# Another order for the attention steps of a fused attention and scan kernel

## The reference, cut to what matters

```
def _attn(a, sin, cos, ga, ba, gb, bb, Wq, Wkv, Wo, bo):
    an = _ln(a, ga, ba)
    bn = _ln(a, gb, bb)
    q = an @ Wq
    k, v = jnp.split(bn @ Wkv, 2, axis=-1)
    ...
    q = _rope(q, sin, cos)
    k = _rope(k, sin, cos)
    dots = jnp.einsum('bhid,bhjd->bhij', q, k)
    attn = jax.nn.softmax(dots, axis=-1)
    out = jnp.einsum('bhij,bhjd->bhid', attn, v)
    ...
    return jax.nn.elu(out @ Wo + bo)
...
return x + (xi + xj) / 2
```

## Time and profile before

| | us |
|---|---|
| median of 3 runs | 327.38 |
| lowest, highest | 326.32, 327.53 |
| the profiled execution | 327.32 |
| its span, first to last instruction | 325.2 |
| first scores, unit 0 | 22.66 |
| first scores of unit 6, of unit 14 | 70.61, 132.12 |
| POOL's first `a_msk` of the scan | 183.10 |

### The profile page before, as it was taken

How to read it: one execution, slowest core, us unless ns; L and a number is a source line. 1 busy time by engine, 2 the same in 40 slices (tenths; PEclk the granted TensorE clock), 3 DMA queues, 4 the chain that set the end, 5 groups by cost and what they waited for, 6 DMA issues and landing times.

```text
span 325.2 us, 7775 instructions
## 1 busy us (share of the span) xinstructions
PE 236.3 (73%) x3138; PEld 141.6 (44%) x3138; DVE 206.1 (63%) x333; ACT 173.1 (53%) x298; POOL 126.1 (39%) x104
## 2 busy tenths in 40 slices
PE   0386977958676865754865799997999848956764
PEld 0153644545444443533565165643544424434331
DVE  2696885828474755754374796999767965483422
ACT  2253655637574757446535844566557337723380
POOL 2416364405444242710040494754796832300000
PEclk9999978969997999795596999998999989997555
DMA  7611010243213133304045300000000000011002
GB/s 179 229 67 65 34 35 33 76 105 84 56 43 67 35 67 81 83 3 85 11 94 112 75 2 2 2 3 3 2 2 2 2 0 2 2 39 29 1 0 65
DMA packets 34243, 15.26 MB, mean 47 GB/s; under 512 B 31008, under 2 KB 31520, under 8 KB 34080
## 3 DMA queue, kind: packets, MB, share of 16 engines
q1 hardware_dynamic: 32480, 13.67, 16.7%
q10 hardware_dynamic: 1728, 1.10, 1.4%
HBM read 5.42 MB, written 2.10 MB: 23 GB/s over the span
## 4 chain that ended last, share of the span: by engine, by line
PE 36%; DVE 31%; ACT 16%; issue 13%; DMA 2%; ACTq 1%; DVEq 0%
PE ring L560 14%; PE score L560 9%; DVE s_max L1043 5%; PE ring L565 5%; DVE s_cen L1047 3%; PE p_turn L560 3%; PE oz L560 2%; DVE mix L1134 2%; DVE ln_s L837 2%; DVE rot_sin L1000 2%; DMA back<-x 2%; DVE rot_cos L1000 2%; DVE ln_v L857 2%; DVE xhat L872 2%; ACT wo_b L1250 2%
## 5 line engine op out<-in xcount | busy, mean ns | idle before, releaser
L1520 POOL TENSOR_TENSOR a_msk<-dt_fin,c_sb 128x512 f32<-128x512 f32 x32 | 40.0, 1251 | 25.0 <-DVE dt_fin L975 15.2
L1043 DVE TENSOR_REDUCE s_max<-score 128x16 f32<-128x1024 f32 x16 | 19.6, 1223 | 26.6 <-PE score L560 26.6
L1134 DVE TENSOR_TENSOR mix<-dec,g_m 128x512 f32<-128x512 f32 x32 | 31.5, 988 | 2.2 <-ACT dec L1377 1.5
L1295 ACT ACTIVATE prob_t<-p_turn 128x512 f32<-128x512 f32 x32 | 17.5, 592 | 25.2 <-PE p_turn L565 25.2
L880 POOL TENSOR_TENSOR k_rot<-rot_cos,rot_swap 128x512 f32<-128x512 f32 x7 | 8.9, 1270 | 43.3 <-DMA rot_swap<-rot_sin 39.0
L1505 POOL TENSOR_TENSOR dtx<-xv,dt_fin 64x512 f32<-64x512 f32 x16 | 19.8, 1240 | 13.2 <-PE p_turn L560 12.3
L1303 ACT ACTIVATE prob<-s_cen 128x1024 f32<-128x1024 f32 x16 | 16.9, 1057 | 13.9 <-DVE s_cen L1047 13.8
L560 PE MATMUL score<-a_msk,c_sb 128*128 128x512 f32 x44 | 24.3, 634 | 0.0
L560 PE MATMUL score<-k_bd,q_rot 32*64 32x128 f32 x512 | 22.9, 329 | 0.0
L560 PEld LDWEIGHTS p_turn<-mix,dtx 128*32 128x32 f32 x512 | 11.0, 109 | 27.4 <-issue 14.6
L892 POOL TENSOR_SCALAR k_bd<-k_rot,c_sb 128x512 f32<-128x512 f32 x14 | 22.1, 1588 | 0.7
(11 more groups left out here) (177 smaller groups left out, 567.8 us busy)
## 6 DMA issues: line engine op xcount, KB each, us to landing
rot_swap<-rot_sin SPq DMA_DIRECT2D x32, 128.0 KB, 2.1
p_sb<-params SPq DMA_DIRECT2D x1, 1520.0 KB, 9.7
x_tok<-x SPq DMA_DIRECT2D x16, 64.0 KB
attention_j_turned<-y_tok SPq DMA_DIRECT2D x16, 64.0 KB, 2.2
back<-attention_j_turned SPq DMA_DIRECT2D x16, 64.0 KB, 2.5
ut_a<-u SPq DMA_DIRECT2D x8, 126.0 KB, 2.8
ut_b<-u SPq DMA_DIRECT2D x8, 124.0 KB, 3.1
ut_b<-u SPq DMA_DIRECT2D x8, 122.0 KB, 3.2
```

The lines of the kernel that those rows point to most:

```text
L1043: v.tensor_reduce(s_max[:, n % 2, :], sc, AX, ALU.max).then_inc(s_maxed, 1)
L1134: v.tensor_tensor(mix[:, e % LAPS, :, :], dec[:, e % LAPS, :, :], wide(g_m[:, e // 4 % 2, e % 4, :], SSM_H), ALU.mult)\
L1295: a.activation(prob_t[:, e % 2, 4 * hp:4 * hp + 4, :].rearrange("p k n -> p (k n)"), PT[hp], ACT.Identity)\
L1520: gp.tensor_tensor(a_msk[:, m % LAPS, :, :], deep(dt_fin[:, 0, SSM_H * m:SSM_H * (m + 1)], GRID), wide(cst("tri"), SSM_H), ALU.mult).then_ ...
```

## The change

```
-ATT_STEPS = 25
+ATT_STEPS = 26
-XT_STEP = (13, 15, 17, 19)
-UT_STEP = (15, 17, 19, 21)
-XP_STEP = (17, 17, 18, 18, 20, 20, 21, 21)
+XT_STEP = (16, 17, 18, 20)
+UT_STEP = (18, 19, 20, 22)
+XP_STEP = (19, 19, 20, 20, 21, 21, 22, 22)
...
-        if odd:
-            uses = [("wo", g - 1), ("k", g + 2), ("yt", g - 2), ("vt", g + 1)]
+        elif odd:
+            a, b, c = [("vt", g + 1)], [("q", g + 2)], []
         else:
-            uses = [("q", g + 1), ("v", g + 1)]
+            a, b, c = [("wo", g - 2)], [("v", g + 1)], [("k", g + 2), ("yt", g - 3)]
...
-DT_STEP = 22
+DT_STEP = 23
...
                     last.then_inc(scored, 1)
+                for use in att_slots[n][0]:
+                    att_use(use)
...
-                for use in att_steps[n][:1]:
+                for use in att_slots[n][1]:
                     att_use(use)
...
-                for use in att_steps[n][1:]:
+                for use in att_slots[n][2]:
                     att_use(use)
...
-            ln_vector_b(v, 1)
             v.wait_ge(sin_signed, 1)
...
-                if use == ("k", 0):
+                if use == ("q", 0):
+                    ln_vector_b(v, 1)
                     ln_vector_c(v, 1)
-                if use == ("q", 0):
...
-                e = n - 1
+                e = n - 2
                 if 0 <= e < UNITS:
...
                     v.tensor_tensor(o_t[:, g % 2, CW // 2 * u:CW // 2 * (u + 1)], OUT, z_inv[:, e % 2, :], ALU.mult).then_inc(o_ready, 1)
+                if n < UNITS:
+                    v.wait_ge(s_maxed, n + 1)
...
+                    v.tensor_tensor(s_cen[:, n % 2, :, :], sc, deep(s_max[:, n % 2, :], GRID), ALU.subtract)\
+                        .then_inc(s_centred, 1)
...
-                if n % 2 == 0 and 1 <= n // 2 < ATT_CHUNKS:
-                    att_use(("vt", n // 2))
+                for use in att_slots[n][0] + att_slots[n][1]:
+                    att_use(use)
...
-                for use in att_steps[n]:
-                    if use[0] != "vt":
-                        att_use(use)
+                for use in att_slots[n][2]:
+                    att_use(use)
...
             copy_xn(0)
+            gp.wait_ge(mid_in, 16)
+            scale_weights(1)
+            gp.memset(v_bd[:, :, :, :], 0.0).then_inc(v_zeroed, 1)
             copy_xn(1)
```

More of the change, by code:

```diff
@@ L63 @@
 FOLD_STEP = 4
-XT_STEP = (13, 15, 17, 19)
-UT_STEP = (15, 17, 19, 21)
-XP_STEP = (17, 17, 18, 18, 20, 20, 21, 21)
+XT_STEP = (16, 17, 18, 20)
+UT_STEP = (18, 19, 20, 22)
+XP_STEP = (19, 19, 20, 20, 21, 21, 22, 22)
 def attention_uses():
-    steps = {-1: [("xr", 0), ("k", 0), ("q", 0), ("xr", 1), ("v", 0), ("vt", 0), ("k", 1)]}
+    steps = {-1: ([("xr", 0), ("k", 0), ("q", 0), ("xr", 1), ("v", 0), ("vt", 0)], [], [])}
     for n in range(ATT_STEPS):
         g, odd = divmod(n, 2)
-        if odd:
-            uses = [("wo", g - 1), ("k", g + 2), ("yt", g - 2), ("vt", g + 1)]
-        else:
-            uses = [("q", g + 1), ("v", g + 1)]
-        steps[n] = [(kind, c) for kind, c in uses if 0 <= c < (CHUNKS if kind == "yt" else ATT_CHUNKS)]
-        if n in (0, 2):
-            steps[n].append(("xr", 2 + n // 2))
+        if n == 0:
+            a, b, c = [("k", 1)], [], []
+        elif n == 1:
+            a, b, c = [("xr", 2), ("q", 1)], [("v", 1)], [("k", 2), ("xr", 3)]
+        elif n == 2:
+            a, b, c = [("vt", 1), ("q", 2)], [("v", 2)], [("k", 3)]
+        elif odd:
+            a, b, c = [("vt", g + 1)], [("q", g + 2)], []
+        else:
+            a, b, c = [("wo", g - 2)], [("v", g + 1)], [("k", g + 2), ("yt", g - 3)]
+        a, b, c = ([(kind, k) for kind, k in uses if 0 <= k < (CHUNKS if kind == "yt" else ATT_CHUNKS)] for uses in (a, b, c))
         if n == FOLD_STEP:
[L83 to L87, removed]
+            c.append(("fold", 0))
+        c += [("ut", q) for q in range(CHUNKS) if UT_STEP[q] == n]
+        c += [("xt", q) for q in range(CHUNKS) if XT_STEP[q] == n]
+        c += [("xp", k) for k, at in enumerate(XP_STEP) if at == n]
+        steps[n] = (a, b, c)
     return steps
@@ L151, in build @@
     lo, n_cols = offsets(COLS)
-    att_steps = attention_uses()
+    att_slots = attention_uses()
+    att_steps = {n: [use for slot in att_slots[n] for use in slot] for n in att_slots}
     ssm_before, ssm_steps = ssm_uses()
@@ L1030, in _ @@
                     q_sum(v, 0)
-                    ln_vector_b(v, 2)
                     v.wait_ge(bias_made, 2)
                     v.tensor_copy(b_att[:, 3:6], oz[:, 3:6]).then_inc(bias_here, 1)
-            ln_vector_c(v, 2)
             for n in range(ATT_STEPS):
@@ L1043, in _ @@
                     v.tensor_reduce(s_max[:, n % 2, :], sc, AX, ALU.max).then_inc(s_maxed, 1)
[L1044 to L1055, removed]
-                for use in att_steps[n]:
-                    if use[0] in ("k", "q"):
-                        att_use(use)
-                e = n - 1
+                e = n - 2
                 if 0 <= e < UNITS:
@@ L1065, in _ @@
                     v.tensor_tensor(o_t[:, g % 2, CW // 2 * u:CW // 2 * (u + 1)], OUT, z_inv[:, e % 2, :], ALU.mult).then_inc(o_ready, 1)
+                if n < UNITS:
+                    v.wait_ge(s_maxed, n + 1)
+                    if n >= 2:
+                        v.wait_ge(exped, n - 1)
+                    v.tensor_tensor(s_cen[:, n % 2, :, :], sc, deep(s_max[:, n % 2, :], GRID), ALU.subtract)\
+                        .then_inc(s_centred, 1)
+                if n == 1:
+                    ln_vector_b(v, 3)
+                for use in att_steps[n]:
+                    if use[0] in ("k", "q"):
+                        att_use(use)
+                    if use == ("q", 1):
+                        ln_vector_c(v, 3)
                 if n == 0:
+                    ln_vector_b(v, 2)
+                    ln_vector_c(v, 2)
                     v.wait_ge(xa_in[3], 32)
                     ln_vector_a(v, 3)
-                if n == 1:
-                    ln_vector_b(v, 3)
-                    ln_vector_c(v, 3)
+                g, odd = divmod(n, 2)
+                if odd and 0 <= g - 2 < ATT_CHUNKS:
+                    c = g - 2
+                    v.wait_ge(wo_biased, c + 1)
+                    v.scalar_tensor_tensor(y_t[:, c // CHUNKS, c % CHUNKS, :], wo_e[:, :], 1.0, wo_b[:, :], ALU.min, ALU.add)\
+                        .then_inc(y_ready, 1)
                 for use in att_steps[n]:
@@ L1286, in _ @@
                 att_use(use)
-            ln_scalar_b(a, 2)
             for n in range(ATT_STEPS):
@@ L1296, in _ @@
                             .then_inc(p_copied, 1)
-                if n % 2 == 0 and 1 <= n // 2 < ATT_CHUNKS:
-                    att_use(("vt", n // 2))
+                for use in att_slots[n][0] + att_slots[n][1]:
+                    att_use(use)
+                if n == 1:
+                    ln_scalar_b(a, 3)
                 if n < UNITS:
@@ L1312, in _ @@
                     a.activation(z_inv[:, e % 2, :], z_log[:, e % 2, :], ACT.Exp, scale=-1.0).then_inc(z_inverted, 1)
-                for use in att_steps[n]:
-                    if use[0] != "vt":
-                        att_use(use)
+                for use in att_slots[n][2]:
+                    att_use(use)
                 if n == 0:
+                    ln_scalar_b(a, 2)
                     ln_scalar_a(a, 3)
-                if n == 1:
-                    ln_scalar_b(a, 3)
                 if n == FOLD_STEP:
@@ L1449, in _ @@
             gp.tensor_scalar(sin_s[0][:, :], par("sin_j"), cst("swap_sign"), None, ALU.mult).then_inc(sin_signed, 1)
-            gp.memset(v_bd[:, :, :, :], 0.0).then_inc(v_zeroed, 1)
-            gp.wait_ge(mid_in, 16)
-            scale_weights(1)
             def rotary(g):
```

## The result

| | before | changed |
|---|---|---|
| median, us | 327.45 (4 runs, 326.32 to 329.58) | 335.94 (4 runs, 332.70 to 337.42) |
| ratio to before | | 1.024, 95% interval 1.014 to 1.033 |
| profiled execution, its span | 327.32, 325.2 | 336.71, 334.6 |

The change makes the kernel 8.5 us slower. The forecast was 329.6 with a range of 321 to 337: the sign and the range held, the size was too small.

The account below looks back on a forecast made before the run. PE's queue was taken to be held by drains of shared banks, no engine being over three quarters busy. Start -0.6, middle -0.1 and end +3.0 gave +2.3, from 327.32 to 329.6 us, range 321 to 337.

Parts of the forecast that it names:

- Start: Stretch up to the scores of unit 6: 70.0 us against 70.6, so -0.6, bounds -2 and +2.
- The wait that replaces the one removed: SP's swap of q stands behind its wait for y_turned and four writes, holding even units' scores to S+14.9 or later.
- The chain as forecast: From even scores' start S: y_tok ends S+8.2, four issues 2.61, swap 2.68 (3.1 taken), POOL's sum 1.28, hand-overs 0.1.
- The size of the middle: Units 6 to 14: four pairs of steps at 15.35 us, 61.4 against 61.5, so -0.1.
- slow matmuls at the head of each pair too: Rival: after PE's wait for q, slow matmuls add 2.3 us a pair; with slow end +16.7, 344 us; chance 0.06.
- the swap: Two DMAs for q right behind four writes, first issue to POOL's start: 3.1 us taken, between 2.68 and 4.05.
- the pair without the hold: Rival: SP's wait doesn't bind, a pair takes 12.4 us by the engines' lists; -9.5, 317.8 us; chance 0.13.
- The end: Unit 14 to a_msk: 54 us against 51.0, so +3.0 (0 to +8), as xt, ut and xp now follow attention.
- the walk at the fast rate: Chain from unit 14's scores to a_msk with all matmuls at the fast rate: 51 us.
- the forecast's hold: Likeliest case: SP's writes hold the swap of q, pairs take 15.35 us; 329.6 us in all; chance 0.47.
- the end at the slow rate: Rival: unit 14 to a_msk with slow matmuls takes 59 us; +7.3 in all, 334.6 us; chance 0.16.
- slow throughout: Rival: slow matmuls at each pair's head, 9.4 us in four pairs, and in the end; 344 us; chance 0.06.

Follow-up runs that it names:

- the moved line: Changed kernel with SP's swap of q of chunk 4+g put before the wait for y_turned and its four writes: 313.29 us, ratio 0.958 to the kernel before.
- the old order with the swap first: Kernel before, with SP's swap of q likewise put ahead of the wait for y_turned and the four writes: 331.75 us, ratio 1.015.

## Why the prediction was right or wrong

**Start.** Right: -0.6 forecast, -0.7 measured, unit 2 at 42.2 forecast and 41.65 measured.

**The wait that replaces the one removed.** Right in mechanism and place, shown by the moved line. The prediction had no row of a later DMA held by a wait in SP's list; the swap at 95.06, its data ready at 85.96, is one. The chain as forecast: `y_tok` done at S+8.2, measured S+7.8 in the pairs with a fast head (77.73 from 69.92, 92.33 from 84.52); writes 2.6 forecast, 2.7 with the gap; POOL's sum 1.26; the hand-overs 0.1.

**The size of the middle.** Forecast -0.1, measured +4.9. (The terms as listed, 8.2 + 2.61 + 3.1 + 1.28 + 0.1, are 15.29 and not 15.35, 61.2 for four; the 0.06 are about what the gaps between them took.) Two terms of the sum. The larger is the clock at the head: I had given "slow matmuls at the head of each pair too" 0.06 and kept it out of the sum. Two of the four pairs had it (units 10 and 12), and there `y_tok` ended at S+10.4, 2.6 later than in the other two (2.3 in that rival): 5.2 us. The smaller is the swap: 3.1 forecast, measured from its first issue to POOL 2.73, 3.98, 2.80 and 4.31, in the mean 3.46: 1.4 us in four. Against them stand four times 0.4 us by which `y_tok` came earlier. 5.2 + 1.4 - 1.6 = 5.0, and that is the difference to the forecast (66.4 to 61.4).

The step that failed is the one that left the clock to a rival: the sum priced the wait for q and put the slow matmuls behind it at nothing. The text had both halves in hand, 3 us of waiting ahead of each head and the slow rate of the same matmuls, and took the wait as harmless, because before the rate had not followed the gaps. The runs with spare matmuls show that in this kernel filling the wait keeps the head fast. In the kernel before, PE's waits in the pairs were pieces of 0.2 to 2.9 us, and here it is one of 3.3 to 4.9. It is tempting to make a rule of that, but the rows don't bear one out: the old order with the swap first had a slow head in all four pairs behind pieces of 2.2 to 2.9 and 0.7 us, and the wait of 3.26 ahead of unit 8 here was followed by 1.10. The rule that the prediction quotes from the Trainium skill, page "TensorE: Matmul & The Clock Gate", section "Loop structure matters more than you think", is that a long wait before every group makes the group run cold. Three of the four waits here agree with it, 1.98 after 4.51, 3.33 and 4.88 us (the wait is for POOL, which waits for a DMA); the fourth doesn't, and shorter waits had slow groups behind them too.

**What would have been.** The forecast put the pair without the hold at 12.4; it took 11.27. Most of it is in the odd step: `y_tok` was done at S+7.8 and not 8.2, the transposes began at 8.4 and not 9.0, the outputs ended at 11.3 and not 12.1, and the next scores followed them at once.

**The end.** Forecast +3.0 out of 0 to +8, measured +5.6. The order of events was that of the forecast, each some 1 to 6 us late against the walk at the fast rate: last outputs at 14.0 instead of 12.4 after unit 14, ut0 at 24.3 instead of 23.3, xp0 at 33.0 instead of 31.4, ut2 at 39.4 instead of 36.3, ut3 at 49.6 instead of 44, `a_msk` at 56.6 instead of 51. The chain of the changed kernel (start us, us, what):

```profile
159.91 0.72 ACT wo_b L1258
160.68 1.98 PE ring L570 x8
162.68 0.70 DVE x_tok L1013
...
169.35 3.88 PE ring L565 x16
...
175.79 1.94 PE ring L570 x8
177.73 5.68 PE ring L565 x32
183.94 0.60 DVE ln_v L864
```

ut0 waits for `wo_b` of wo7, as forecast, and the xps stand on the chain, with 3.88 us for two at the slow rate and 5.68 for four mostly at it. The term that was too small is the share of the slow rate (0.72 granted); 54, taken near the middle between fast and slow, was short by 2.6. The 5.6 us by which the walk at the fast rate was exceeded lie in three places (the two pieces between them are off by -0.6 and +0.6). 1.6 are in the last outputs: the head of unit 14 is slow, behind the wait of 4.88 us, and with the swap first, where it is fast, the outputs come at 11.9 and the whole end is 1.4 shorter. So this part belongs to the hold and not to the later steps. 1.5 are from xp0 to ut2 (6.4 instead of 4.9), and 2.5 from ut2 to ut3 (10.2 instead of 7.7). In the run with spare matmuls in the end, where the xps from ut2 to ut3 took the fast rate, that last piece was 7.7, as forecast; the first two xps were still mostly slow there, and the piece around them 6.1.

**The sum.** -0.7 + 4.9 + 5.6 - 0.4 = +9.4, forecast +2.3. The case that came true is the forecast's hold together with most of "the end at the slow rate" and half of "slow throughout". That 335.9 lies within the range is in part luck: two of the four pairs (17.2 and 18.8 us) were longer than the 16.3 that the forecast allowed at most, and the upper edge of 337 was made of a slow end with a late swap, without slow heads. The two rivals were treated as separate cases with small chances, but the slow head of unit 14 counts in the end, so the one made the other likelier.

## What to carry to other kernels

When uses are moved against each other on the compute engines, walk every issuing queue whose list is written out by hand as well: one line left in its old place in SP's list turned a gain of 14 us into a loss of 8.5. Where a change puts a wait of several us ahead of a group of matmuls, put the slow rate of that group into the sum and not among the rivals: here it followed three waits of four and cost 2.6 us in each of the two pairs that had it. Moving the same line was no gain in the old order, where it delayed the writes and what waited for them: the place of a line in SP's list is right only for one order of the others. Where a reorder disappoints, look in the waits for an engine that has been idle for long and yet is waited for (POOL, 9.5 us idle, PE behind it): the cause sits in the queue that feeds it.

## What the runs showed of the hardware

Spare matmuls on constants in PE's idle time made the kernel 6.4 us faster by the medians in one place (335.9 to 329.6) and 4.6 in another (311.5 to 306.9), where only 2.2 us lie in the stretch that has them. The same 32 score matmuls behind the same waits of 2.21 and 0.69 us took 1.10 in one pair and 1.98 in another of the kernel before. Two DMAs within SBUF took 2.7 us from their first issue to the engine that waits for them with an idle queue, once 4.05, and 2.7 to 4.5 right behind four writes to DRAM (2.73, 3.98, 2.80, 4.31 in the changed kernel; 2.73, 3.51, 4.43, 2.74 with three spare matmuls, 2.74, 3.29, 4.46, 3.71 with six). What makes the long ones long isn't shown.
